# Taking the offset of the third normalisation on GpSimd instead of VectorE, one operation per tile of rows

## The chip, the cores and the metric

The kernel runs on one core of one Trainium2 chip. The metric is the time of one launch on the device, in microseconds (us). The kernel before has a median of 659.78 us in three runs (659.73 to 660.92). Engines are named as the profile names them: PE is TensorE (PEld its weight loads), DVE is VectorE, ACT is ScalarE, POOL is GpSimd, SP is the engine whose queue issues nearly all transfers.

## The reference, cut to what matters

A block of a transformer over 32 batches of 256 rows with 256 columns. An attention part of the mLSTM kind (8 heads, gates with cumulative sums, decay matrices) is added to x, and then a feed-forward part, which is where the third normalisation stands:

```python
x = x + tanh(g_xattn[0]) * L0_xattn_ref(layernorm(x), ctx_1024, ctx_1024, ...)   # ends in a second normalisation
x = x + tanh(g_ffn[0]) * L0_ffn_ref(layernorm(x), W_fc, W_proj)                  # layernorm(x): the third one
# layernorm(x) = (x - mean) / sqrt(var + 1e-5)
# L0_ffn_ref:  h = square(relu(x @ W_fc.T));  y = h @ W_proj.T;  five steps of a spiking neuron on y, mean of the spikes
```

## The kernel before, in words

A batch is 256 rows, kept as two tiles of 128 rows (`ST` is 2). Every engine has an order of work written out by hand: a start, and then a loop over `n in SLOTS` (n = 1 to 9), each turn of which handles four batches; I call one turn a slot. Work for a batch that doesn't exist is skipped, so that the last slots are partly empty. Engines wait for one another only on semaphores, and each engine works strictly in its own order: an instruction that waits holds up all that is behind it on its engine.

The third normalisation of batch b takes these steps. `x1_step` (DVE) makes x after the attention part. `ln3_stats` (DVE, L904) takes mean and variance into `mv3`. `ln3_rstd` (ACT, L915) makes 1/std of both tiles in two small activations (L370 and L371). `ln3_offset` (L926) makes minus mean times 1/std: on DVE, one instruction on 128x2 elements through `offset_of` (L374), which the first normalisation uses as well, on 128x4. `ln3_apply` (ACT, L934) makes the normalised rows `x1ln` with two activations (L942), which read the offset as their bias. `x2_T` (PE, L463) transposes them, `x2_hi_step` (ACT, L962) and `x2_lo_step` (DVE, L968) split them in two parts, and the feed-forward products follow: `z_step` (PE, L997), `relu_step` (ACT, L1007), `square` (ACT, L1019 and L1020), `square_lo` (POOL, L1040), `y_step` (PE, L1057), `spikes_step` (DVE, L1071 and L1075).

Other steps that the prediction speaks of:

- `am_split(n + 3, 0 to 3)` splits the gate rows of the next four batches in three bf16 parts: steps 0 and 2 on ACT (L635), steps 1 and 3 on POOL (L637). Only when step 3 (`am_part`) is done does SP go on with `load_a_rows` and `load_m_rows` (L650, six small transfers a batch).
- SP's order behind them in a slot is: rows for batches 4n+4 and 4n+5, `load_values(4n + 5)`, `stack_heads(4n + 5)` (L513, eight transfers that stack the heads of q and k), `load_k` and `load_values`, rows for 4n+6, `load_k`, `stack_heads(4n + 6)`, and then a store. (The last lines of one slot and the first of the next.)
- On POOL `k_hi(4n + 10)` (L428) waits until `stack_heads(4n + 6)` has landed, since it writes over what that reads. Behind it on POOL stand `v_lo_step(4n + 5)` (L456), `square_lo(2n + 1, 7)` (L1040) and `c_lo_step(4n + 5, 1)` (L746).
- `state(4n + 5)` (PE, L808) waits for `v_lo_step(4n + 5)`. `arg(4n + 6, 1)` (PE, L702) waits for the activation `decay_exp(4n + 6, 0)` (ACT, L728), which stands on ACT behind `ln3_apply(4n + 4)` and `x2_hi_step(4n + 3)`.
- `c_lo_step` (POOL, L746), `k_lo`, `k_weigh` and `state_lo` (POOL) are further elementwise work of the attention part.

Of the kernel before, what the change touches and what calls it, by code (L numbers as in the profile page):

```python
# [34 lines left out]
def build_block(nc, x, ctx_rows, ctx_cols, g_both, gate_w, gate_b, ln_scale, w_fc_t, w_proj_t, out):  # L35
# [37 lines left out]
    with ExitStack() as ctx:  # L73
# [852 lines left out]
        def ln3_offset(e, b):  # L926
            if not 0 <= b < B:
                return
            e.wait_ge(sem("ln3_rstd"), b + 1)
            if b - 2 >= 0:  # L930
                e.wait_ge(sem("x1ln"), b - 1)
            offset_of(e, off3[b % 2], mv3[b % 2], rstd3[b % 2]).then_inc(sem("ln3_offset"), 1)

        def ln3_apply(e, b):  # L934
            if not 0 <= b < B:
# [475 lines left out]
        def vector_program(e):  # L1411
            setup_rows(e, 1)
            setup_cols(e)
            ln1_stats(e, 0)
            ln1_stats(e, 1)
            ln1_offset(e, 0)
            setup_gates(e)
            ln1_stats(e, 2)
            q_lo(e, 0)
            q_lo(e, 1)  # L1420
            ln1_stats(e, 3)
            setup_rows(e, 0)
            gate_pre(e, 0)
            gate_cumsum(e, 0)
            ln1_offset(e, 1)
            gate_cummax(e, 0)
            ln1_stats(e, 4)
            am_split(e, 0, 1)
            ln1_stats(e, 5)
            am_split(e, 0, 3)  # L1430
            split_wfc_lo(e, 0)
            gate_pre(e, 1)
            setup_own(e)
            gate_cumsum(e, 1)
            gate_cummax(e, 1)
            q_lo(e, 2)
            am_split(e, 1, 1)
            ln1_offset(e, 2)
            q_lo(e, 3)
            cmul(e, 0, 0)  # L1440
            cmul(e, 0, 1)
            am_split(e, 1, 3)
            cmul(e, 0, 2)
            state_own(e, 0)
            ln1_stats(e, 6)
            q_lo(e, 4)
            split_wpr_lo(e, 0)
            split_wfc_lo(e, 1)
            cmul(e, 0, 3)
            gate_pre(e, 2)  # L1450
            gate_cumsum(e, 2)
            cmul(e, 1, 0)
            gate_cummax(e, 2)
            h_norm(e, 0)
            ln2_stats(e, 0)
            cmul(e, 1, 1)
            x1_step(e, 0)
            cmul(e, 1, 2)
            state_own(e, 1)
            ln3_stats(e, 0)  # L1460
            q_lo(e, 5)
            ln3_offset(e, 0)
            cmul(e, 1, 3)
            ln1_stats(e, 7)
            split_wpr_lo(e, 1)
            x2_lo_step(e, 0)
            ln1_offset(e, 3)
            cmul(e, 2, 0)
            h_norm(e, 1)
            cmul(e, 2, 1)  # L1470
            ln2_stats(e, 1)
            q_lo(e, 6)
            cmul(e, 2, 2)
            x1_step(e, 1)
            ln3_stats(e, 1)
            state_own(e, 2)
            cmul(e, 2, 3)
            ln3_offset(e, 1)
            ln1_stats(e, 8)
            q_lo(e, 7)  # L1480
            h_norm(e, 2)
            x2_lo_step(e, 1)
            ln2_stats(e, 2)
            cmul(e, 3, 0)
            x1_step(e, 2)
            cmul(e, 3, 1)
            gate_pre(e, 3)
            gate_cumsum(e, 3)
            gate_cummax(e, 3)
            ln1_stats(e, 9)  # L1490
            ln3_stats(e, 2)
            ln3_offset(e, 2)
            state_own(e, 3)
            cmul(e, 3, 2)
            ln1_offset(e, 4)
            spikes_step(e, 0, 0)
            spikes_step(e, 0, 1)
            cmul(e, 3, 3)
            spikes_step(e, 0, 2)
            spikes_step(e, 0, 3)  # L1500
            x2_lo_step(e, 2)
            spikes_step(e, 0, 4)
            cmul(e, 4, 0)
            h_norm(e, 3)
            cmul(e, 4, 1)
            ln2_stats(e, 3)
            cmul(e, 4, 2)
            x1_step(e, 3)
            cmul(e, 4, 3)
            q_lo(e, 8)  # L1510
            out_step(e, 0)
            for n in SLOTS:
                state_own(e, 4 * n)
                ln3_stats(e, 4 * n - 1)
                cmul(e, 4 * n + 1, 0)
                ln3_offset(e, 4 * n - 1)
                h_norm(e, 4 * n)
                ln2_stats(e, 4 * n)
                cmul(e, 4 * n + 1, 1)
                q_lo(e, 4 * n + 5)  # L1520
                x1_step(e, 4 * n)
                cmul(e, 4 * n + 1, 2)
                ln3_stats(e, 4 * n)
                cmul(e, 4 * n + 1, 3)
                ln3_offset(e, 4 * n)
                ln1_stats(e, 4 * n + 6)
                state_own(e, 4 * n + 1)
                x2_lo_step(e, 4 * n - 1)
                ln1_stats(e, 4 * n + 7)
                spikes_step(e, 2 * n - 1, 0)  # L1530
                cmul(e, 4 * n + 2, 0)
                spikes_step(e, 2 * n - 1, 1)
                ln1_offset(e, 2 * n + 3)
                x2_lo_step(e, 4 * n)
                spikes_step(e, 2 * n - 1, 2)
                spikes_step(e, 2 * n - 1, 3)
                spikes_step(e, 2 * n - 1, 4)
                cmul(e, 4 * n + 2, 1)
                out_step(e, 2 * n - 1)
                h_norm(e, 4 * n + 1)  # L1540
                q_lo(e, 4 * n + 6)
                ln2_stats(e, 4 * n + 1)
                cmul(e, 4 * n + 2, 2)
                x1_step(e, 4 * n + 1)
                ln3_stats(e, 4 * n + 1)
                state_own(e, 4 * n + 2)
                cmul(e, 4 * n + 2, 3)
                ln1_stats(e, 4 * n + 8)
                ln3_offset(e, 4 * n + 1)
                q_lo(e, 4 * n + 7)  # L1550
                h_norm(e, 4 * n + 2)
                cmul(e, 4 * n + 3, 0)
                ln2_stats(e, 4 * n + 2)
                gate_pre(e, n + 3)
                gate_cumsum(e, n + 3)
                gate_cummax(e, n + 3)
                x2_lo_step(e, 4 * n + 1)
                x1_step(e, 4 * n + 2)
                ln3_stats(e, 4 * n + 2)
                state_own(e, 4 * n + 3)  # L1560
                cmul(e, 4 * n + 3, 1)
                ln3_offset(e, 4 * n + 2)
                ln1_stats(e, 4 * n + 9)
                spikes_step(e, 2 * n, 0)
                spikes_step(e, 2 * n, 1)
                cmul(e, 4 * n + 3, 2)
                spikes_step(e, 2 * n, 2)
                spikes_step(e, 2 * n, 3)
                spikes_step(e, 2 * n, 4)
                cmul(e, 4 * n + 3, 3)  # L1570
                ln1_offset(e, 2 * n + 4)
                x2_lo_step(e, 4 * n + 2)
                out_step(e, 2 * n)
                cmul(e, 4 * n + 4, 0)
                h_norm(e, 4 * n + 3)
                cmul(e, 4 * n + 4, 1)
                ln2_stats(e, 4 * n + 3)
                cmul(e, 4 * n + 4, 2)
                x1_step(e, 4 * n + 3)
                cmul(e, 4 * n + 4, 3)  # L1580
                q_lo(e, 4 * n + 8)
# [228 lines left out]
        def gpsimd_program(e):  # L1810
# [31 lines left out]
            c_lo_step(e, 1, 2)  # L1842
            state_lo(e, 1)
            k_hi(e, 6)
            k_lo(e, 6)
            k_weigh(e, 2)
            c_lo_step(e, 1, 3)
# [7 lines left out]
            square_lo(e, 0, 1)  # L1855
            c_lo_step(e, 2, 2)
            state_lo(e, 2)
            c_lo_step(e, 2, 3)
            k_lo(e, 7)
            square_lo(e, 0, 2)  # L1860
# [9 lines left out]
            square_lo(e, 0, 6)  # L1870
            am_split(e, 3, 1)
            c_lo_step(e, 3, 1)
            am_split(e, 3, 3)
            square_lo(e, 0, 7)
            k_weigh(e, 4)
# [14 lines left out]
            k_hi(e, 9)  # L1890
            state_lo(e, 4)
            k_lo(e, 8)
            square_lo(e, 1, 3)
            v_lo_step(e, 5)
            v_hi_step(e, 6)
# [6 lines left out]
            c_lo_step(e, 5, 1)  # L1902
            square_lo(e, 1, 6)
            square_lo(e, 1, 7)
            c_lo_step(e, 5, 2)
            c_lo_step(e, 5, 3)
            k_weigh(e, 6)
# [15 lines left out]
            c_lo_step(e, 6, 3)  # L1923
            k_weigh(e, 7)
            for n in SLOTS:
                square_lo(e, 2 * n, 3)
                v_lo_step(e, 4 * n + 3)
                square_lo(e, 2 * n, 4)
# [3 lines left out]
                square_lo(e, 2 * n, 7)  # L1932
                am_split(e, n + 3, 1)
                c_lo_step(e, 4 * n + 3, 0)
                am_split(e, n + 3, 3)
                c_lo_step(e, 4 * n + 3, 1)
                square_lo(e, 2 * n + 1, 0)
# [16 lines left out]
                c_lo_step(e, 4 * n + 4, 3)  # L1954
                state_lo(e, 4 * n + 4)
                k_weigh(e, 4 * n + 5)
                k_hi(e, 4 * n + 9)
                c_lo_step(e, 4 * n + 5, 0)
                v_hi_step(e, 4 * n + 5)
# [5 lines left out]
                k_hi(e, 4 * n + 10)  # L1965
                v_lo_step(e, 4 * n + 5)
                square_lo(e, 2 * n + 1, 7)
                c_lo_step(e, 4 * n + 5, 1)
                c_lo_step(e, 4 * n + 5, 2)
                state_lo(e, 4 * n + 5)  # L1970
# [74 lines left out]
```

## Time and profile before

| what | us |
|---|---|
| median of three runs | 659.78 |
| the profiled execution itself | 662.98 |
| its span, first to last instruction | 661.2 |
| PE busy | 589.5 (89%) |
| DVE busy | 542.4 (82%) |
| POOL busy | 485.6 (73%) |
| ACT busy | 484.4 (73%) |
| chain that ended last, share of PE, DVE, ACT, POOL | 51%, 10%, 7%, 7% |
| the same, SP's queue, transfers, issue | 4%, 2%, 10% |

The granted clock of PE was 0.972 on average over the span. All rows of the trace come from the profiled execution, 3.2 us longer than the median. In a timeline a row is: start in us, duration in us, engine, line, operation, output and inputs, shapes, how many; in square brackets the idle time of the engine before it, and what ended that. In this profile a POOL instruction's duration overlaps the next one's start by some 0.04 us when they follow without a gap.

### The profile page before, as it was taken

How to read it: one execution, taken by the hardware profiler on the slowest of the kernel's cores; microseconds unless marked ns; L12 is line 12 of the kernel's file. 1: busy time of each engine (PE TensorE's matmuls, PEld its weight loads, DVE VectorE, ACT ScalarE, POOL GpSimd, SP SyncE). 2: the span in 40 equal slices, each digit the busy share in tenths (PEclk: the TensorE clock that was granted, in tenths of full speed). 3: DMA queues.
4: the chain of work that ended last, by engine and by line, in shares of the span. 5: the costliest groups of instructions: out<-in, count | busy, mean ns of one | idle time of the engine just before them, and what ended most of it. 6: DMA issues, size and time to landing. Idle time of an engine off the chain costs nothing.

```text
span 661.2 us, 17665 instructions
## 1 busy us (share of the span) xinstructions
PE 589.5 (89%) x6032; PEld 483.9 (73%) x6032; DVE 542.4 (82%) x1222; ACT 484.4 (73%) x1011; POOL 485.6 (73%) x531
## 2 busy tenths in 40 slices
PE   1265887799999999999999999999999999999795
PEld 0155776778787878787788878787878777787684
DVE  4878787889989998899989998999888998958522
ACT  4555777678787888788878878788878867676463
POOL 6157678867996969787897799787969788675232
PEclk9996799999999999999999999999999999999898
DMA  8915553845276335916573538642680556300000
GB/s 262 225 52 115 97 115 70 176 83 96 83 156 169 74 91 147 208 26 139 115 186 60 96 110 155 159 86 80 150 207 18 97 101 148 63 2 33 1 33 32
DMA packets 73192, 71.33 MB, mean 108 GB/s; under 512 B 8720, under 2 KB 68752, under 8 KB 73104
## 3 DMA queue, kind: packets, MB, share of 16 engines
q1 hardware_dynamic: 71888, 70.00, 47.3%
q8 instruction: 49, 0.80, 0.6%
q14 instruction: 39, 0.32, 0.2%
q10 hardware_dynamic: 1216, 0.21, 0.2%
HBM read 27.44 MB, written 8.39 MB: 54 GB/s over the span
## 4 chain that ended last, share of the span: by engine, by line
PE 51%; DVE 10%; issue 10%; ACT 7%; POOL 7%; SPq 4%; DMA 2%; POOLq 0%; ACTq 0%; DVEq 0%
PE z_ps L997 16%; PE y_ps L1057 16%; PE arg_ps L702 3%; PE qk_ps L717 3%; POOL sq_lo L1040 3%; DVE spikes L1075 3%; PE misc_ps L463 2%; SPq L650 2%; PE misc_ps L529 2%; SPq L513 2%; ACT sq_hi L1019 1%; POOL c_lo L746 1%; PE pv_ps L766 1%; PE pv_ps L764 1%; PE pv_ps L841 1%
## 5 line engine op out<-in xcount | busy, mean ns | idle before, releaser
L1040 POOL TENSOR_TENSOR sq_lo<-w_raw,sq_hi 128x512 fp32r<-128x512 f32 (+1 forms) x96 | 113.0, 1178 | 66.2 <-ACT w_raw L1020 66.1
L746 POOL TENSOR_TENSOR c_lo<-decay 128x512 bf16<-128x512 f32 x128 | 132.5, 1042 | 22.4 <-DVE decay L736 22.2
L997 PE MATMUL z_ps<-x_hi,wfc_hi 128*128 128x512 f32 (+1 forms) x288 | 115.7, 402 | 5.9 <-ACT w_raw L1007 4.1
L1057 PE MATMUL y_ps<-sq_hi,wpr_hi 128*128 128x512 f32 (+1 forms) x288 | 115.1, 400 | 1.1 <-POOL sq_lo L1040 1.1
L997 PE MATMUL z_ps<-x_hi,wfc_lo 128*128 128x512 f32 (+1 forms) x288 | 107.2, 372 | 0.0
L997 PE MATMUL z_ps<-x_lo,wfc_hi 128*128 128x512 f32 (+1 forms) x288 | 107.2, 372 | 0.0
L1057 PE MATMUL y_ps<-sq_lo,wpr_hi 128*128 128x512 f32 (+1 forms) x288 | 106.8, 371 | 0.0
L1057 PE MATMUL y_ps<-sq_hi,wpr_lo 128*128 128x512 f32 (+1 forms) x288 | 106.6, 370 | 0.0
L736 DVE TENSOR_TENSOR decay<-qk_ps,decay 128x512 f32<-128x512 f32 x128 | 87.1, 680 | 18.5 <-PE qk_ps L717 14.4
L728 ACT ACTIVATE decay<-arg_ps,lqk_col 128x512 f32<-128x512 f32 x128 | 86.5, 676 | 19.7 <-PE arg_ps L705 19.1
L1040 POOL TENSOR_TENSOR sq_lo<-relu,sq_hi 128x512 fp32r<-128x512 f32 (+1 forms) x48 | 56.3, 1173 | 37.9 <-ACT relu L1020 35.2
L1075 DVE SCALAR_TENSOR_TENSOR spikes<-y_ps,spikes 128x1024 bf16<-128x1024 f32 (+1 forms) x72 | 79.4, 1103 | 1.7
L1007 ACT ACTIVATE w_raw<-z_ps 128x512 f32<-128x512 f32 (+1 forms) x96 | 52.4, 545 | 29.6 <-PE z_ps L997 28.7
L997 PEld LDWEIGHTS z_ps<-x_hi,wfc_hi 128*128 128x128 f32 x288 | 55.0, 191 | 17.5 <-ACT w_raw L1007 4.8
L997 PEld LDWEIGHTS z_ps<-x_hi,wfc_lo 128*128 128x128 f32 x288 | 55.0, 191 | 10.0
L1057 PEld LDWEIGHTS y_ps<-sq_hi,wpr_lo 128*128 128x128 f32 x288 | 54.5, 189 | 10.0
L1057 PEld LDWEIGHTS y_ps<-sq_hi,wpr_hi 128*128 128x128 f32 x288 | 54.6, 190 | 9.4 <-POOL sq_lo L1040 2.1
L1019 ACT ACTIVATE sq_hi<-w_raw 128x512 fp32r<-128x512 f32 (+1 forms) x96 | 55.9, 582 | 6.2 <-PE y_ps L1057 5.3
L997 PEld LDWEIGHTS z_ps<-x_lo,wfc_hi 128*128 128x128 f32 x288 | 55.2, 192 | 6.7
L1057 PEld LDWEIGHTS y_ps<-sq_lo,wpr_hi 128*128 128x128 f32 x288 | 54.8, 190 | 6.4
L1020 ACT ACTIVATE w_raw<-w_raw 128x512 f32<-128x512 f32 (+1 forms) x96 | 56.3, 587 | 3.0
L702 PE MATMUL arg_ps<-m_rows,a_rows 128*128 128x128 bf16 x512 | 51.8, 226 | 5.7 <-ACT decay L728 5.2
(139 smaller groups left out, 1686.2 us busy)
## 6 DMA issues: line engine op xcount, KB each, us to landing
x_in<-x SPq DMA_DIRECT2D x32, 256.0 KB, 3.5
kT_in<-ctx_cols SPq DMA_DIRECT2D x32, 256.0 KB, 3.8
v_in<-ctx_rows SPq DMA_DIRECT2D x32, 256.0 KB, 3.2
k_stack<-kT_hi SPq DMA_DIRECT2D x64, 128.0 KB, 3.4
k_stack<-kT_lo SPq DMA_DIRECT2D x64, 128.0 KB, 3.7
q_stack<-qT_hi SPq DMA_DIRECT2D x64, 128.0 KB, 4.0
q_stack<-qT_lo SPq DMA_DIRECT2D x64, 128.0 KB, 4.2
out<-w_raw SPq DMA_DIRECT2D x32, 256.0 KB, 3.6
```

Of the source, the lines that this page charges most:

```text
L702: e.matmul(arg_ps[:, cols], a_rows[b % NAM][:, h, tok], m_rows[b % NAM][:, h, tok], start=(cols.start == 0), stop=False, skip_group_check= ...
L717: ins = e.matmul(qk_ps[:, cols], k_stack[slot][:, g, c, tok], q_stack[slot][:, g, c, tok], start=True, stop=True)
L728: e.activation(decay[i % NUN][:, :], arg_ps[:, :], ACT.Exp, bias=lqk_col[:, :]).then_inc(sem("decay"), 1)
L736: e.tensor_tensor(decay[i % NUN][:, :], qk_ps[:, :], decay[i % NUN][:, :], ALU.mult).then_inc(sem("cmul"), 1)
L746: e.tensor_tensor(c_lo[i % NCH][:, :], c, top(c), ALU.subtract).then_inc(sem("c_lo"), 1)
L997: ins = e.matmul(z_ps[:, tokens(q)], lhsT, rhs, start=(n == 0), stop=(n == len(terms) - 1))
L1007: e.activation(relu[n % NRE][:, tokens(q)], z_ps[:, tokens(q)], ACT.Relu).then_inc(sem("relu"), 1)
L1019: link(e, "scalar", e.activation(sq_hi[n % NSQ][:, tokens(q)], r, ACT.Square))
L1020: e.activation(r, r, ACT.Square).then_inc(sem("square"), 1)
L1040: e.tensor_tensor(sq_lo[n % NSQ][:, tokens(q)], relu[n % NRE][:, tokens(q)], sq_hi[n % NSQ][:, tokens(q)].bitcast(fp32), ALU.subtract).the ...
L1057: ins = e.matmul(y[:, c, :], w[:, j, c * P:(c + 1) * P], h, start=(j == 0 and i == 0 and (c == 0 or whole)), stop=(j == FT - 1 and i == 2) ...
L1075: ins = e.scalar_tensor_tensor(count, y, THETA[n], count, ALU.is_gt, ALU.add)
```

## The change

`ln3_offset` leaves DVE's order and goes into POOL's. Its one instruction on 128x2 becomes one `tensor_scalar` per tile of rows, each on 128x1, with 1/std as a per-partition scalar. What it waits for stays the same: 1/std of its batch, and the `x1ln` of two batches ago. The diff, shortened where slots repeat the pattern:

```diff
@@ ln3_offset
             e.wait_ge(sem("ln3_rstd"), b + 1)
             if b - 2 >= 0:
                 e.wait_ge(sem("x1ln"), b - 1)
-            offset_of(e, off3[b % 2], mv3[b % 2], rstd3[b % 2]).then_inc(sem("ln3_offset"), 1)
+            for t in range(ST):
+                ins = e.tensor_scalar(off3[b % 2][:, t:t + 1], mv3[b % 2][:, t, 0:1], rstd3[b % 2][:, t:t + 1], -1.0,
+                                      ALU.mult, ALU.mult)
+            ins.then_inc(sem("ln3_offset"), 1)
@@ vector_program: all seven calls go, three in the start and four in the loop
                 ln3_stats(e, 4 * n - 1)
                 cmul(e, 4 * n + 1, 0)
-                ln3_offset(e, 4 * n - 1)
                 h_norm(e, 4 * n)
...
                 state_own(e, 4 * n + 3)
                 cmul(e, 4 * n + 3, 1)
-                ln3_offset(e, 4 * n + 2)
@@ gpsimd_program, start
             k_hi(e, 6)
+            ln3_offset(e, 0)
             k_lo(e, 6)
...
             am_split(e, 3, 1)
             c_lo_step(e, 3, 1)
+            ln3_offset(e, 2)
             am_split(e, 3, 3)
...
@@ gpsimd_program, loop
             for n in SLOTS:
+                ln3_offset(e, 4 * n + 1)
                 square_lo(e, 2 * n, 3)
...
                 am_split(e, n + 3, 1)
                 c_lo_step(e, 4 * n + 3, 0)
+                ln3_offset(e, 4 * n + 2)
                 am_split(e, n + 3, 3)
                 c_lo_step(e, 4 * n + 3, 1)
...
                 state_lo(e, 4 * n + 4)
                 k_weigh(e, 4 * n + 5)
+                ln3_offset(e, 4 * n + 3)
                 k_hi(e, 4 * n + 9)
...
                 k_hi(e, 4 * n + 10)
                 v_lo_step(e, 4 * n + 5)
                 square_lo(e, 2 * n + 1, 7)
+                ln3_offset(e, 4 * n + 4)
                 c_lo_step(e, 4 * n + 5, 1)
```

In DVE's order the calls were for batches 0, 1 and 2 in the start and for 4n-1, 4n, 4n+1 and 4n+2 in the loop; in POOL's they are for batches 0 to 4 in the start and for 4n+1 to 4n+4 in the loop.

## Rows read from the trace of the kernel before

**Rows 1.** Groups by line and form: busy us, mean ns | idle us before, releaser.
```profile
L428 POOL TENSOR_SCALAR kT_hi<-kT_in 128x512 bf16<-128x512 f32 x32 | 21.0, 656 | 27.1 <-DMA kT_in<-ctx_cols 14.9 <-DMA q_stack<-qT_lo 12.2
...
L374 DVE SCALAR_TENSOR_TENSOR off<-mv,rstd 128x2 f32<-128x2 f32 x32 | 19.0, 593 | 6.5 <-ACT rstd L371 6.4
```
**Rows 2.** Groups of POOL by form, for the fixed part of an instruction.
```profile
L746 POOL TENSOR_TENSOR c_lo<-decay 128x512 bf16<-128x512 f32 x128 | 132.5, 1042 | 22.4 <-DVE decay L736 22.2
...
L794 POOL TENSOR_TENSOR kw_lo<-kw 128x256 bf16<-128x256 f32 x32 | 20.1, 629 | 0.2
...
L2039 POOL MEMSET const-bfloat16-1.0<- 128x1 bf16 x1 | 0.1, 102 | 0.0
```
**Rows 3.** Timeline of POOL around am_part in slots 3 and 4.
```profile
310.42 1.03 POOL L746 TENSOR_TENSOR c_lo<-decay 128x512 bf16<-128x512 f32 x1
311.42 1.16 POOL L637 TENSOR_TENSOR am_part<-am_rest,am_part 32x512 bf16<-32x512 f32 x1
...
315.00 1.28 POOL L1040 TENSOR_TENSOR sq_lo<-w_raw,sq_hi 128x512 fp32r<-128x512 f32 x1 [1.42 <-ACT w_raw L1020]
...
382.54 1.16 POOL L637 TENSOR_TENSOR am_part<-am_rest,am_part 32x512 bf16<-32x512 f32 x1
```
**Rows 4.** Timeline of ACT, 1/std and x1ln of batch 4n+2 in slot 3.
```profile
311.34 0.21 ACT L371 ACTIVATE rstd<-lnv 128x2 f32<-128x2 f32 x1
...
312.63 1.10 ACT L942 ACTIVATE x1ln<-x,off,rstd 128x256 f32<-128x256 f32 x2 [0.44 <-DVE off L374]
```
**Rows 5.** Timeline of DVE, the offsets of batch 0 and of 4n+2 in slot 3.
```profile
65.28 0.38 DVE L374 SCALAR_TENSOR_TENSOR off<-mv,rstd 128x2 f32<-128x2 f32 x1 [1.09 <-ACT rstd L371]
...
311.57 1.02 DVE L374 SCALAR_TENSOR_TENSOR off<-mv,rstd 128x2 f32<-128x2 f32 x1 [0.19 <-ACT rstd L371]
```
**Rows 6.** Timeline of SP's queue, slot 3: first and last of the rows of 38 issues.
```profile
312.64 2.12 SPq L650 DMA_DIRECT2D a_rows<-am_part  x3
...
337.57 1.25 SPq L513 DMA_DIRECT2D q_stack<-qT_lo  x2
```
**Rows 7.** Timeline of POOL, slot 3, from k_hi(4n+10) on.
```profile
342.76 0.62 POOL L428 TENSOR_SCALAR kT_hi<-kT_in 128x512 bf16<-128x512 f32 x1 [1.34 <-DMA q_stack<-qT_lo]
343.34 1.12 POOL L456 TENSOR_TENSOR v_lo<-v_in,v_hi 128x512 bf16<-128x512 f32 x1
344.43 1.27 POOL L1040 TENSOR_TENSOR sq_lo<-relu,sq_hi 128x512 fp32r<-128x512 f32 x1
345.66 2.04 POOL L746 TENSOR_TENSOR c_lo<-decay 128x512 bf16<-128x512 f32 x2
```
**Rows 8.** Timeline of PEld: inter, state and arg in slot 3.
```profile
319.73 0.10 PEld L841 LDWEIGHTS pv_ps<-state_f,qT_hi 128*128 128x128 bf16 x1 [0.59 <-POOL s_lo L829]
...
344.54 0.10 PEld L808 LDWEIGHTS pv_ps<-v_hi,kw 128*128 128x128 bf16 x1
...
348.15 0.23 PEld L702 LDWEIGHTS arg_ps<-m_rows,a_rows 128*128 128x128 bf16 x4 [0.28 <-issue]
```
**Rows 9.** Timeline of ACT, x1ln of batch 4n+4 in slots 3 and 5.
```profile
345.75 1.10 ACT L942 ACTIVATE x1ln<-x,off,rstd 128x256 f32<-128x256 f32 x2 [0.82 <-DVE off L374]
...
488.68 1.10 ACT L942 ACTIVATE x1ln<-x,off,rstd 128x256 f32<-128x256 f32 x2 [1.32 <-DVE off L374]
```
**Rows 10.** Timeline of PEld: state and arg in slot 5.
```profile
487.47 0.10 PEld L808 LDWEIGHTS pv_ps<-v_hi,kw 128*128 128x128 bf16 x1 [0.61 <-issue]
...
490.95 0.24 PEld L702 LDWEIGHTS arg_ps<-m_rows,a_rows 128*128 128x128 bf16 x4 [0.31 <-issue]
```
**Rows 11.** Timeline of POOL, slot 5: v_lo and what follows it.
```profile
486.28 1.12 POOL L456 TENSOR_TENSOR v_lo<-v_in,v_hi 128x512 bf16<-128x512 f32 x1
487.36 1.27 POOL L1040 TENSOR_TENSOR sq_lo<-w_raw,sq_hi 128x512 fp32r<-128x512 f32 x1
```
**Rows 12.** Timeline of POOL in the start and in slot 7.
```profile
71.73 1.04 POOL L746 TENSOR_TENSOR c_lo<-decay 128x512 bf16<-128x512 f32 x1 [2.79 <-DVE decay L736]
...
613.55 1.29 POOL L1040 TENSOR_TENSOR sq_lo<-relu,sq_hi 128x512 fp32r<-128x512 f32 x1 [1.50 <-ACT relu L1020]
```

More of the change, by code:

```diff
@@ L1461, in vector_program @@
             q_lo(e, 5)
-            ln3_offset(e, 0)
             cmul(e, 1, 3)
@@ L1477, in vector_program @@
             cmul(e, 2, 3)
-            ln3_offset(e, 1)
             ln1_stats(e, 8)
@@ L1491, in vector_program @@
             ln3_stats(e, 2)
-            ln3_offset(e, 2)
             state_own(e, 3)
@@ L1524, in vector_program @@
                 cmul(e, 4 * n + 1, 3)
-                ln3_offset(e, 4 * n)
                 ln1_stats(e, 4 * n + 6)
@@ L1548, in vector_program @@
                 ln1_stats(e, 4 * n + 8)
-                ln3_offset(e, 4 * n + 1)
                 q_lo(e, 4 * n + 7)
@@ L1857, in gpsimd_program @@
             state_lo(e, 2)
+            ln3_offset(e, 1)
             c_lo_step(e, 2, 3)
@@ L1892, in gpsimd_program @@
             k_lo(e, 8)
+            ln3_offset(e, 3)
             square_lo(e, 1, 3)
@@ L1904, in gpsimd_program @@
             square_lo(e, 1, 7)
+            ln3_offset(e, 4)
             c_lo_step(e, 5, 2)
```

## The prediction, made before the changed kernel was run

> **What bounds the kernel now.** I read the page first: the chain that ended last is half PE, with 10% DVE, 7% ACT and 7% POOL, so PE sets the time but is handed short waits by the others. Then the groups by form. The offset on DVE is 128x2 elements, yet costs 593 ns on average, 19.0 us in all [rows 1]; the reader is to see that it starts at 311.57 and ends at 312.59, with POOL's am_part at 312.58 [rows 3, 5]. That looks like a price that the change takes away. So the third view was the timeline of each engine over one slot (n = 3, from about 297 to 368 us), and there the question was which wait is passed from slot to slot.
>
> A slot is 71.12 us long (am_part at 311.42 and at 382.54 [rows 3]). The loop that closes on itself is this. When am_part ends at 312.58, SP starts at 312.64 and issues 38 transfers one behind the other, with gaps of at most 0.12 us, until the last of stack_heads(4n+6) at 338.82 [rows 3, 6]. That lands at about 342.7, and k_hi(4n+10) on POOL had waited 1.34 us for it [rows 7]. Behind it stands v_lo(4n+5), which ends at 344.46, and at 344.54 PE starts state(4n+5) [rows 7, 8]. In slot 5 v_lo ends at 487.40 and state starts at 487.47, after 0.61 us in which PE's loads had stood [rows 10, 11]. From there PE works without a gap into the gate transposes, and ACT and POOL take it to the next am_part. So am_part is on the loop, and a delay of it is passed on one to one, because SP has nothing to give back. This holds for n = 1 to 5: in slot 6 batch 34 doesn't exist, so nothing waits for the transfers, and from slot 7 on there is no am_part.
>
> **The price of one new instruction.** Call it c, from start to start. The trace has no 128x1 tensor_scalar on POOL. Two elementwise forms differ in width alone: 1042 ns at 512 elements and 629 ns at 256 [rows 2], which is 1.61 ns an element and 216 ns at none; less the 0.04 us by which neighbours overlap that is 0.18 us. Bounds from both sides: 0.10 us, a memset of 128x1 [rows 2], and 0.62 us, the tensor_scalar on 512 elements, 656 ns less 0.04 [rows 1]. I take 0.18, since the operation reads and writes as those two do; 0.30 I hold possible for the per-partition scalar.
>
> The Trainium skill, "GPSIMD Engine Reference", section "Performance pitfalls for Q7 kernels", says that many small read commands cost about 102 cycles each and do not overlap. At the 1.2 GHz of the same page that is an estimate of 0.085 us for each of the two reads here; if they came on top of half the fixed price, c would be near 0.27 and the sum below 6.0 us in place of 4.2. No row shows a POOL instruction this small that reads, so I leave it in the upper half of the range.
>
> **Part 1, offset(4n+2) before am_part.** POOL reaches it when c_lo ends, at 311.42 in slot 3. But 1/std ends at 311.55 [rows 4], and DVE, which was waiting for it, started at 311.57 [rows 5]; POOL can start at about 311.6. Then two instructions, then am_part: it starts 0.18 + 2c later, 0.54 us. Queued behind it on POOL are c_lo(4n+3,1) and square_lo(2n+1,0); the latter had an idle of 1.42 us before it [rows 3], so these lose nothing. What isn't covered is am_part itself, and through it SP. Five slots: 0.90 + 10c = 2.7 us.
>
> **Part 2, offset(4n+4) behind square_lo(2n+1,7).** On DVE it ran beside POOL's work; on POOL it comes when square_lo is done, at 345.66 [rows 7]. It ends at 345.66 + 2c + 0.04, and with 0.05 us to reach ACT, x1ln(4n+4) starts at 345.75 + 2c, where it was 345.75 [rows 9]. In slot 5 the start is 487.36 + 1.23 + 0.09 + 2c = 488.68 + 2c, where it was 488.68 [rows 9, 11]. Late next on ACT are x_hi and the decay, and for that decay PE's arg(4n+6,1) waits: 2.27 us after x1ln in slot 5, with 0.31 us of standing [rows 9, 10]. In slot 3 arg started at 348.15, 2.40 us after x1ln, so 0.13 us are spare [rows 8, 9]. Price: 2c in slot 5, 2c - 0.13 in slot 3; I take the mean, 2c - 0.07, for each of five slots: 10c - 0.3 = 1.5 us. This lies behind state on PE, and so adds to part 1.
>
> **Part 3, the other two of each slot.** Offset(4n+1) and offset(4n+3) find 1/std ready or within 0.1 us, and push POOL by 2c = 0.36 us. The second is covered by the 1.34 us for which k_hi(4n+10) waits anyway [rows 7], the first by a wait of square_lo for ACT, of the kind of the 1.42 us [rows 3]. Nothing; without that cover each would cost 0.36 us a slot, 1.8 us over five.
>
> **Part 4, start and end.** In the start offset(0) holds POOL from about 64.4 until 1/std is there at about 65.3 [rows 5], and k_lo(6), k_weigh(2) and c_lo(1,3) behind it move by 0.9 + 2c, some 1.2 us; an idle of 2.79 us before 71.73 takes that in [rows 12]. In slot 7 offset(31) makes square_lo(15,5) wait for 1/std of the last batch, some 0.9 us; before the next square_lo stands an idle of 1.50 us [rows 12]. I count nothing for both, and 1.2 and 0.9 us if the cover fails.
>
> **Part 5, what DVE gets back.** 19.0 us of busy time and 6.5 us of waits [rows 1]. None of it is on the loop above, where DVE doesn't stand between am_part and state. x1ln(4n+2) gets earlier, by the 0.44 us that ACT had waited [rows 4], but what comes of it is used on PE before state, where PE now has time to spare. Nothing.
>
> **The sum.** 0.90 + 10c + 10c - 0.3 = 0.6 + 20c, with c = 0.18 4.2 us. The profiled execution took 662.98 us, so 667.2; times 659.78 / 662.98 = 0.9952 for the median, 664.0 us. With c = 0.10 the sum is 2.6 and the time 662.4; with 0.30, 6.6 and 666.4; with 0.62, 13.0 and 672.7.
>
> **Rival A, faster.** The place is s_lo before inter(4n+3): PE stood 0.59 us for it [rows 8], and it hangs on square_lo(2n+1,0), which hangs on ACT behind x1ln(4n+2). The offset was blocked on DVE for the rest of am_part (1.02 us for 128x2 [rows 5]); on POOL it ends at 311.6 + 0.40 = 312.0, and x1ln starts 0.44 us earlier [rows 4]. If that decided in six slots, it would be 2.6 us: 657.2. For it speaks that the printed chain goes this way; against it that in slots 3 and 5 state starts within 0.08 us of v_lo's end, which has nothing to do with x1ln. It decides if the transfers land by their own queue and not by when SP issued them. The block is what the Trainium skill, "SBUF — State Buffer", section "Who interferes with whom", states: a DVE instruction with two SBUF inputs contends with a GpSimd instruction that reads SBUF, and the second to start waits for all of the first. The trace agrees [rows 3, 5]; by this rule alone the change gains.
>
> **Rival B, no change.** The delay of am_part is absorbed between SP and POOL: the last transfer took 3.9 us from its issue to k_hi [rows 6, 7], and if transfers queue there, an issue 0.5 us later may land at the same time. Then only part 2 is left, and against it part of rival A's gain: between -1 and +1.2 us, about 659.8.
>
> **Rival C, much slower.** A POOL instruction with a per-partition scalar costs as much as a wide one, or the cover of part 3 fails: 668 to 673. Against it, that no group of POOL shows a fixed price over 0.2 us.
>
> **Rival D**, the change doesn't do what it says: DVE's offset gone, yet x1ln starting no later or earlier anywhere. The two tiles' offsets are the same numbers, and I see no way to it; 1%, as no change.
>
> **Chances.** Forecast (c from 0.10 to 0.35) 64%, rival A 11%, rival B 14%, rival C 10%, D 1%. Changes within 0.2%, 1.3 us, are about what a measurement of this kernel can't tell from none. Of the forecast nearly all lies above that, and a part of B lies on either side. Slower by over 0.2%: 0.74; within 0.2%: 0.14; faster: 0.12. The forecast's own range is 662.4 to 667.3; the range for 8 times in 10 reaches down through half of B and up into C: 659.4 to 668.6.
>
> **What would show it right or wrong.** Right: POOL has 64 instructions on 128x1 of 0.2 us; am_part starts 0.4 to 0.7 us later after the end of the c_lo before it; the slots are 71.9 to 72.1 us long; k_hi(4n+10) still waits for the transfers; PEld stands 0.3 us or more before state in slots 1 to 5. DVE's busy time falls by some 19 us without use. Wrong: slots of 71.1 us or less, state starting well behind v_lo's end, or the last stack transfer landing where it did relative to the slot.

## The result and the profile after

The changed kernel takes 665.41 us (median of 8 runs, 664.17 to 667.13), the kernel before on the same chips 660.70 (8 runs, 659.73 to 663.89). The ratio is 1.0065, with an interval of 1.0044 to 1.0086, so 4.3 us slower (2.9 to 5.7). The forecast was 664.0, with 4.2 us of difference.

The span of its profiled execution is 665.3 us. From the page of the changed kernel: busy times, the new group on POOL, and the chain that ended last.

```profile
PE 591.3 (89%) x6032; PEld 484.4 (73%) x6032; DVE 526.8 (79%) x1190; ACT 483.5 (73%) x1011; POOL 501.7 (75%) x595
...
PE 32%; SPq 20%; DVE 11%; issue 10%; POOL 7%; ACT 6%; DMA 5%; POOLq 0%; ACTq 0%; DVEq 0%
```

```profile
L933 POOL TENSOR_SCALAR off<-mv,rstd 128x1 f32<-128x1 f32 x64 | 16.0, 265 | 3.9 <-ACT rstd L371 3.4
```

DVE is 15.6 us less busy, and the kernel is slower. POOL has 64 new instructions in 16.0 us, and SP's queue has 20% of the printed chain, where it had 4%.

POOL and ACT in slot 3, the answer to [rows 3, 4, 5]:

```profile
312.80 1.03 POOL L746 TENSOR_TENSOR c_lo<-decay 128x512 bf16<-128x512 f32 x1
314.01 0.50 POOL L933 TENSOR_SCALAR off<-mv,rstd 128x1 f32<-128x1 f32 x2 [0.18 <-ACT rstd L371]
314.47 1.16 POOL L637 TENSOR_TENSOR am_part<-am_rest,am_part 32x512 bf16<-32x512 f32 x1
```
```profile
314.55 1.10 ACT L945 ACTIVATE x1ln<-x,off,rstd 128x256 f32<-128x256 f32 x2
```

The wait is 0.18 us as worked out, and the two instructions take 0.46 us from start to start, so c is 0.23. Am_part starts 1.67 us after c_lo where it was 1.00. ACT no longer waits for the offset.

POOL and ACT behind v_lo(4n+5) in slots 3 and 4, the answer to [rows 7, 9]:

```profile
345.88 0.62 POOL L428 TENSOR_SCALAR kT_hi<-kT_in 128x512 bf16<-128x512 f32 x1 [1.53 <-DMA q_stack<-qT_lo]
346.47 1.11 POOL L456 TENSOR_TENSOR v_lo<-v_in,v_hi 128x512 bf16<-128x512 f32 x1
347.54 1.27 POOL L1043 TENSOR_TENSOR sq_lo<-relu,sq_hi 128x512 fp32r<-128x512 f32 x1
348.79 0.51 POOL L933 TENSOR_SCALAR off<-mv,rstd 128x1 f32<-128x1 f32 x2
...
418.61 1.11 POOL L456 TENSOR_TENSOR v_lo<-v_in,v_hi 128x512 bf16<-128x512 f32 x1
```
```profile
349.33 1.10 ACT L945 ACTIVATE x1ln<-x,off,rstd 128x256 f32<-128x256 f32 x2 [2.09 <-POOL off L933]
...
421.48 1.10 ACT L945 ACTIVATE x1ln<-x,off,rstd 128x256 f32<-128x256 f32 x2 [1.96 <-POOL off L933]
```

And the same place of slot 4 in the kernel before, which the prediction had not read (DVE, POOL and ACT):

```profile
416.12 0.16 DVE L374 SCALAR_TENSOR_TENSOR off<-mv,rstd 128x2 f32<-128x2 f32 x1
```
```profile
415.08 1.12 POOL L456 TENSOR_TENSOR v_lo<-v_in,v_hi 128x512 bf16<-128x512 f32 x1
416.16 1.27 POOL L1040 TENSOR_TENSOR sq_lo<-w_raw,sq_hi 128x512 fp32r<-128x512 f32 x1
```
```profile
416.31 1.10 ACT L942 ACTIVATE x1ln<-x,off,rstd 128x256 f32<-128x256 f32 x2 [0.23 <-DVE off L374]
```

In the changed kernel x1ln(4n+4) starts 1.75 us after v_lo's end in slot 3 and 1.76 in slot 4. Before it was 1.29 in slot 3 (345.75 less 344.46, [rows 7, 9]), where DVE's offset stood until square_lo ended, but only 0.11 in slot 4: there the offset started 0.04 us before square_lo and got through. In slots 2 and 5 it was 1.28, much as in slot 3. In slot 1 it was 0.05: DVE's offset had stood there too, but only until v_lo ended.

**A cleaner measure than the time.** Executions of one kernel scatter by 3 to 8 us from the lowest to the highest, so I cut each slot in two at the end of v_lo(4n+5). Stretch A goes from there to the end of the next am_part, stretch B from the end of am_part to v_lo. In the changed kernel A is 40.38, 40.36, 40.38, 40.38 and 40.39 us, in the kernel before 38.83, 39.28, 39.24, 38.78 and 39.26. There it has two levels, 38.8 and 39.26, 0.45 us apart: the lower one in slots 1 and 4, where x1ln(4n+4) starts at most 0.11 us after v_lo's end, and the upper one where DVE's offset(4n+4) stands until square_lo ends. B scatters, since transfers stand in it. Between the two profiled executions A takes 5 x 1.30 = 6.5 us more, B 5 x 0.70 = 3.5 less, am_part of slot 1 ends 2.5 later, and the rest behind slot 6's is 1.4 shorter: together 4.1, the difference of the spans.

### The profile page after: what moved, and what is told of

Read it like the earlier page. It is cut to its first block, busy times and chain, and to the rows that moved or that the text cites. A ratio compares the mean times of both kernels' runs of the same rounds, so it can differ in the third digit from the quotient of the medians.

```text
span 665.3 us, 17697 instructions
## 1 busy us (share of the span) xinstructions
PE 591.3 (89%) x6032; PEld 484.4 (73%) x6032; DVE 526.8 (79%) x1190; ACT 483.5 (73%) x1011; POOL 501.7 (75%) x595
## 4 chain that ended last, share of the span: by engine, by line
PE 32%; SPq 20%; DVE 11%; issue 10%; POOL 7%; ACT 6%; DMA 5%; POOLq 0%; ACTq 0%; DVEq 0%
PE z_ps L1000 11%; SPq L650 10%; PE y_ps L1060 10%; SPq L513 8%; DVE spikes L1078 6%; DMA q_stack<-qT_lo 4%; POOL sq_lo L1043 2%; PE arg_ps L702 2%; PE qk_ps L717 2%; DVE spikes L1074 1%; PE misc_ps L529 1%; ACT sq_hi L1022 1%; POOL am_part L637 1%; DVE stat L358 1%; ACT x1ln L945 1%
```

## The experiments

The times are differences to the kernel before on the same chip. Each is the ratio on record of the two kernels' runs, less one, times the median before, with its 95% interval; it can differ by up to 1.4 us from the plain difference of the two medians. Most of the intervals reach 1.2 to 1.9 us to either side, so that differences between two rows of the table are less certain than the rows. A and B are means over slots 1 to 5 of one profiled execution each.

| kernel | against before, us | A | B |
|---|---|---|---|
| before | 0 | 39.08 | 32.38 |
| the change | +4.3 (2.9 to 5.7) | 40.38 | 31.68 |
| part 1 alone | +1.9 (0.4 to 3.3) | 39.47 | 32.06 |
| delay of part 1, no offset moved | +1.0 (-0.7 to 2.6) | 39.84 | 31.56 |
| part 2 alone | +3.4 (2.2 to 4.7) | 39.75 | 32.24 |
| change without part 2 | +1.6 (0.3 to 2.9) | 39.73 | 31.77 |
| part 3 alone | -0.5 (-1.5 to 0.5) | 39.32 | 31.94 |
| change, start on DVE | +5.6 (3.7 to 7.5) | 40.36 | 31.83 |
| change, 4n+2 behind am_part | +3.8 (2.4 to 5.3) | 39.77 | 31.96 |
| change, one instruction | +1.1 (-0.3 to 2.6) | 39.72 | 31.65 |
| before, k_hi behind v_lo | +0.3 (-1.3 to 2.0) | 42.14 | 29.93 |
| change, k_hi behind v_lo | +3.0 (1.3 to 4.7) | 42.44 | 29.83 |
| before, two instructions on DVE | -2.0 (-3.1 to -0.8) | 39.08 | 32.33 |
| before, offset on ACT | +7.0 (5.4 to 8.7) | 40.45 | 31.71 |

**Offset(4n+2) behind am_part.**

```diff
                 c_lo_step(e, 4 * n + 3, 0)
-                ln3_offset(e, 4 * n + 2)
                 am_split(e, n + 3, 3)
+                ln3_offset(e, 4 * n + 2)
```

> As the change, but offset(4n+2) stands behind am_part on POOL. The trace of the change gives c = 0.23 us for one new instruction, and its am_part starts 0.64 us (0.18 of wait and 2c) behind the c_lo before it, in five slots that count. Theory (the loop over am_part, SP, the stack transfers and v_lo): 5 x 0.64 = 3.2 us of the change's 4.3 to 4.7 go away, so about 1.2 us above the kernel before. x1ln(4n+2) then starts some 0.7 us later than before, and that must cost nothing. Rival 1 (every new instruction on POOL costs its own length wherever it stands): no gain, 4.5 us above the kernel before. Rival 2 (x1ln(4n+2) leads to s_lo and the inter product on PE): the gain is eaten, 3 us or more above before.

It came out 3.8 us slower than before, no gain that can be measured. A falls by 0.61 as expected, but B grows by 0.28, and POOL in slot 3 shows why:

```profile
344.16 0.62 POOL L428 TENSOR_SCALAR kT_hi<-kT_in 128x512 bf16<-128x512 f32 x1 [0.28 <-PE misc_ps L529]
```

K_hi no longer waits for the transfers here: in slots 3 to 5 they have landed when POOL comes. X1ln(4n+2) starts 1.67 us after am_part's start, where it was 1.21, and what hangs on it brings POOL late by itself. The theory's 1.2 us is refuted. The time fits rival 2, and the trace shows its way: a second chain is nearly as long as the one over SP. Rival 1's 4.5 us lies inside the interval too; it falls with the kernels that follow.

**Part 1 alone, part 2 alone, the change without part 2, part 3 alone.** These call one function with the POOL form (`_g`) or one with the old DVE form (`_v`), each at the place of its engine. Where engines alternate, each waits for the offset of the batch before:

```diff
+            if b - 1 >= 0:
+                e.wait_ge(sem("ln3_offset"), b)
@@ part 1 alone, gpsimd_program; all others stay ln3_offset_v on DVE
+                ln3_offset_g(e, 4 * n + 2)
@@ part 2 alone, gpsimd_program, and ln3_offset_g(e, 4) in the start
+                ln3_offset_g(e, 4 * n + 4)
@@ the change without part 2, vector_program
+                ln3_offset_v(e, 4 * n)
@@ part 3 alone, gpsimd_program, and ln3_offset_g(e, 3) in the start
+                ln3_offset_g(e, 4 * n + 1)
...
+                ln3_offset_g(e, 4 * n + 3)
```

> As the kernel before, but offset(4n+2) alone is taken on POOL, in front of am_part; all others stay on DVE. Theory: 5 x (0.18 + 2 x 0.23) = 3.2 us slower than before. Rival 1 (each new instruction costs its length anywhere, 4.5 us over 64 of them): 16 of 64, 1.1 us. Rival 2 (the earlier x1ln pays the delay back): 1 us or less, or a gain.

> Only the offsets of batches 4, 8, 12, ... are on POOL, behind square_lo(2n+1,7); all others stay on DVE. This is the missing corner beside part 1 alone, both, and part 3 alone. I measure with the stretch from the end of v_lo(4n+5) to the end of the next am_part, which repeats to some 0.02 us in five slots: 39.08 us before on average, 40.38 after, 39.47 with part 1 alone. Theory (the two parts lie one behind the other on one path): 40.38 less the 0.64 of part 1, so 39.74 in every slot, 0.66 above before, and the time 2 to 3.3 us above before. Rival (the parts overlap, and each alone costs nearly what both do): 40.0 or more and over 3.5 us. Second rival (part 2 matters only when part 1 has made the rest late): 39.3 or less and under 1 us.

> As the change, but the offsets of batches 4, 8, 12, ... (4n+4) are back on DVE at their old place. Theory: part 2 goes away, 5 x 2 x 0.23 - 0.3 = 2.0 us, so about 2.5 us above the kernel before. Rival 1 (by share of instructions): 8 of 32 batches, 1.1 us less, 3.4 above before. Rival 3 (the path behind v_lo has slack of its own for x1ln(4n+4)): no gain, 4.5 above before.

> Only the offsets of batches 3, 5, 7, 9, ... are on POOL, at the places of the change; batches 0, 1, 2 and all 4n+2 and 4n+4 stay on DVE. The prediction counted these at nothing. Theory: within 1 us of the kernel before (with 16 offsets of 0.46 us on POOL, 7.4 us of its time in all, hidden). Rival 1 (an instruction costs its length wherever it stands, 4.5 us for all 32 offsets): half of that, 2.2 us slower.

Part 1 alone cost 1.9 us, where 3.2 was expected; 3.2 lies just inside the interval. Part 2 alone cost 3.4, a little over its range, and its A was 39.75, where 39.74 stood in the expectation. Without part 2 the change costs 1.6 us. Part 3 costs nothing that shows: 15 offsets of 0.46 us lie under waits of POOL. Rival 1, by which an instruction on POOL costs its length anywhere, falls with this: it gave part 2 1.1 us and part 3 2.2, and both lie outside the intervals.

Part 1 alone also moved DVE's offset(4n+4) to another place beside POOL's work. In its trace x1ln(4n+4) starts at most 0.14 us after v_lo's end in all five slots, where in the kernel before that was so in two. So A is at 39.5 throughout, 0.67 above the lower level, but only 0.39 above the mean before. This is slot 2, where the offset had taken 0.79 us before:

```profile
274.54 0.16 DVE L374 SCALAR_TENSOR_TENSOR off<-mv,rstd 128x2 f32<-128x2 f32 x1
```

**The delay without the offset.**

```diff
+        def hold(e, b):
+            e.wait_ge(sem("ln3_rstd"), b + 1)
+            for t in range(ST):
+                e.tensor_scalar(idle2[:, t:t + 1], eps_col[:, :], eps_col[:, :], -1.0, ALU.mult, ALU.mult)
@@ gpsimd_program
+                hold(e, 4 * n + 2)
                 am_split(e, n + 3, 3)
```

> As the kernel before, with all offsets on DVE, but in front of am_part POOL waits for 1/std of batch 4n+2 and runs two tensor_scalar on 128x1 that write a tile which nothing reads. So it has the delay of part 1 and nothing of what DVE gets back. Theory: 3.2 us slower than before, the same as with the real offset there. Rival 2 (what DVE gets back is worth something): this kernel is slower than the one with the real offset, by up to 5 x 0.44 = 2.2 us.

1.0 us, with zero inside the interval and 3.2 outside it, so the delay isn't passed on one to one. But the kernel isn't the delay alone. While POOL waits for 1/std, DVE's offset(4n+2) gets through in front of am_part. It took 1.02 us before, and here in slot 3:

```profile
312.39 0.16 DVE L375 SCALAR_TENSOR_TENSOR off<-mv,rstd 128x2 f32<-128x2 f32 x1
```

X1ln(4n+2) starts 0.02 us before am_part, about as early as with the real offset on POOL (0.08 us behind am_part's start). So this kernel has what DVE gets back as well, and it can't tell rival 2 from the theory. What speaks against a worth of it at this place is the changed kernel's trace: square_lo(2n+1,0) starts 4.10 us after the c_lo before am_part in slot 3, where it was 4.58, and k_hi(4n+10) then waits for the transfers all the same.

**The start back on DVE.**

```diff
@@ the change, vector_program: batches 0, 1 and 2; they go from gpsimd_program
+            ln3_offset_v(e, 0)
...
+            ln3_offset_v(e, 1)
...
+            ln3_offset_v(e, 2)
```

> As the change, but the offsets of batches 0, 1 and 2, in the start, are back on DVE. In the trace of the change am_part of slot 1 is 2.5 us late, where the prediction had counted nothing for the start. Theory: that is real and is kept to the end, so this kernel is some 2 us below the change and 2.5 above before. Rival: it is absorbed later by the waits for the transfers (from am_part to v_lo the change's trace is 0.7 us shorter in a slot): less than 0.7 us below the change.

5.6 us above before (6 runs), so not clearly below the change, and the theory's 2.5 is refuted. That the 2.5 us at slot 1 in the trace of the change are a cost of the start's offsets isn't shown. Over the traces of all the kernels am_part of slot 1 ends between 167.9 and 172.2, and the latest is the kernel with part 2 alone, which has the offsets of batches 0 to 3 on DVE.

**One instruction in place of two.**

```diff
-            for t in range(ST):
-                ins = e.tensor_scalar(off3[b % 2][:, t:t + 1], ...
+            e.tensor_tensor(off3[b % 2][:, :], mv3[b % 2][:, :, 0], rstd3[b % 2][:, :], ALU.mult)
```

> As the change, but POOL makes the offset by one tensor_tensor on 128x2 in place of two tensor_scalar on 128x1; the minus sign is left out. Theory: one instruction of this size costs about 0.25 us, so 0.21 us are saved at each of the two places of a slot, 2.1 us in five slots and 0.4 in the start: about 2 us below the change. Rival (the wait for 1/std and the order, not the length, is the loss): within 0.7 us of the change.

The instruction took 0.15 us from start to start:

```profile
309.92 0.20 POOL L932 TENSOR_TENSOR off<-mv,rstd 128x2 f32<-128x2 f32 x1 [0.17 <-ACT rstd L371]
310.07 1.16 POOL L637 TENSOR_TENSOR am_part<-am_rest,am_part 32x512 bf16<-32x512 f32 x1
```

That is 0.31 less at each of the two places of a slot, and A fell by 0.66. Five slots make 3.3 us, and the time is 3.2 below the change's. So the loss in A scales with the length of these instructions. B stays at 31.65, although am_part is now delayed by 0.33 us and no longer by 0.64.

**K_hi(4n+10) behind v_lo(4n+5)**, in the kernel before and in the changed one.

```diff
-                k_hi(e, 4 * n + 10)
                 v_lo_step(e, 4 * n + 5)
+                k_hi(e, 4 * n + 10)
```

> As the kernel before, but k_hi(4n+10), which waits for the stack transfers of 4n+6, stands behind v_lo(4n+5) on POOL and not in front of it. Theory (the loop over the transfers sets the slot): v_lo(4n+5) no longer waits 1.3 to 2.5 us, state(4n+5) on PE starts up to the 0.6 to 1.2 us earlier for which PE's loads had stood, and five slots give 2 to 3.5 us, so 2 to 3.5 us faster than before. Rival (another chain of nearly the same length, over x1ln(4n+2) and square_lo, holds the slot, as the kernel with the offset behind am_part seems to show): within 1 us of before.

> As the change, with the same move: k_hi(4n+10) behind v_lo(4n+5). Theory: the 0.64 us of delay of am_part per slot is no longer passed on through v_lo to PE's state, and offset(4n+4) comes about 1 us earlier in the slot, since square_lo(2n+1,7) in front of it is reached earlier; 3 to 4 us less than the change, so 0.5 to 1.5 us above the kernel before. Rival (the delay goes on by ACT's x1ln and POOL's own order, not by the transfers): no more than 1 us less than the change, 3.5 us above before.

No gain in the first, and none that is clear in the second. Slots 1 and 2 did get shorter in the first (71.05 and 70.87 us, before 72.01 and 71.22), but slots 4 and 5 took 73.3. The move takes v_lo and PE's state out from behind the transfers, but not square_lo(2n+1,7) and what follows on POOL: in slots 1, 4 and 5 k_hi still waits 1.01, 0.88 and 0.99 us for the transfers, in slots 2 and 3 under 0.1. Who waited for what on PE in slot 4 (us in all, times, longest):

```profile
PEld qk_ps L717 <- issue: 3.9, 12, 1.0
...
PEld y_ps L1086 <- DVE spikes L1075: 1.2, 1, 1.2
```

State(4n+5) no longer stands, but a product of q_stack and k_stack now has an idle of 0.98 us before it, and a `y` product waits 1.2 us for the spikes. In the kernel before PE is busy 70.4 to 70.8 us of each such slot of 71.1 to 72.0, so the gate that the prediction saw was one of several, mostly with less than 1 us between them.

**The form of the change on DVE.**

```diff
@@ the kernel before, ln3_offset, still called on DVE
-            offset_of(e, off3[b % 2], mv3[b % 2], rstd3[b % 2]).then_inc(sem("ln3_offset"), 1)
+            for t in range(ST):
+                ins = e.tensor_scalar(off3[b % 2][:, t:t + 1], mv3[b % 2][:, t, 0:1], rstd3[b % 2][:, t:t + 1], -1.0,
+                                      ALU.mult, ALU.mult)
+            ins.then_inc(sem("ln3_offset"), 1)
```

> As the kernel before, all offsets on DVE at their places, but in the form of the change: two tensor_scalar on 128x1 in place of one scalar_tensor_tensor on 128x2. It tells form from engine. Theory: the loss is POOL's in-order queue and not the form, so this is not slower than before; if one tensor input in place of two keeps DVE from waiting for POOL's running instruction, an offset costs some 0.3 us in all in place of 0.59 on average, x1ln(4n+2) and x1ln(4n+4) start 0.3 to 0.5 us earlier, and it is 1 to 3 us faster than before. Rival (the two instructions are blocked as the one was): same as before within 0.7 us or slower, with a mean of about 0.6 us for the pair.

2.0 us faster than before by the ratio of the runs (0.8 to 3.1); the medians are 659.44 us (11 runs) and 662.29 before. This version beats both kernels. The group, and the activations x1ln(4n+2) of slot 3:

```profile
L933 DVE TENSOR_SCALAR off<-mv,rstd 128x1 f32<-128x1 f32 x64 | 10.5, 205 | 7.6 <-ACT rstd L371 7.3
```
```profile
313.61 1.08 ACT L945 ACTIVATE x1ln<-x,off,rstd 128x256 f32<-128x256 f32 x2
```

No single instruction took more than 0.22 us, where the one before went up to 1.26. X1ln(4n+2) starts 0.66 us after am_part's start, where it was 1.21. In slots 1, 4 and 5 A is 38.80 to 38.84, the lower of the two levels, but its mean is no lower than before, since slot 2 took 39.93: there 1/std itself came late. B is no shorter either (32.33, before 32.38). The profiled execution took 662.26 us, 2.8 more than this kernel's median, so that a trace of a typical execution, and with it the place where the 2.0 us are won, is missing. That it is the stopped offset(4n+4) is what A in the three slots suggests; it isn't shown.

**The offset on ACT.**

```diff
@@ ln3_stats, DVE
+            e.tensor_scalar(nm3[b % 2][:, :], mv3[b % 2][:, :, 0], -1.0, None, ALU.mult).then_inc(sem("ln3_neg"), 1)
@@ ln3_rstd, ACT
+            for t in range(ST):
+                ins = e.activation(off3[b % 2][:, t:t + 1], nm3[b % 2][:, t:t + 1], ACT.Identity,
+                                   scale=rstd3[b % 2][:, t:t + 1])
+            ins.then_inc(sem("ln3_offset"), 1)
```

> As the kernel before, but ACT makes the offset itself, by two activations on 128x1 (minus the mean, times 1/std as scale) right behind 1/std; DVE takes minus the mean behind its statistics. No engine is crossed between 1/std and x1ln. Theory: ACT had waited 0.44 us for DVE's offset in front of x1ln(4n+2) and 0.2 to 1.3 us in front of x1ln(4n+4); two activations take some 0.45 us, so about 0.4 us a slot are won and some 1 us of ACT's time a batch is added elsewhere under cover: 0 to 2 us faster than before. Rival (ACT's queue is on PE's way to work, as the short waits of PE for w_raw show): 1 to 3 us slower.

7.0 us slower. The two places in question are DVE's new instruction and ACT behind it, slot 3:

```profile
346.91 1.04 DVE L916 TENSOR_SCALAR nm<-mv 128x2 f32<-128x2 f32 x1
```
```profile
348.04 0.48 ACT L931 ACTIVATE off<-nm,rstd 128x1 f32<-128x1 f32 x2 [0.60 <-DVE nm L916]
```

The block came back: on 128x2 `tensor_scalar` took 1.04 us beside POOL's square_lo, and 0.48 us of ACT stand behind it. The edit also lets DVE wait for its own statistics before this instruction. How much of the 7 us is ACT's longer queue, how much this block and how much DVE's added work I haven't separated.

## Why the prediction was right, and where it wasn't

- **c.** Taken 0.18, measured 0.23, inside the bounds. The tensor_tensor with two small reads took 0.15 from start to start and 0.20 as recorded. The Trainium skill, "GPSIMD Engine Reference", section "Performance pitfalls for Q7 kernels", has about 102 cycles for each small read command, from which the prediction's estimate was 0.27 for c and 0.17 for two commands alone; these rows neither show such a price nor rule it out.
- **Part 1, the place.** Wait and delay came out as worked out: 0.18 + 2c = 0.64 us, in every slot. SP's first issue starts 0.06 us behind am_part in all slots of both kernels.
- **Part 1, the price.** "A delay of it is passed on one to one, because SP has nothing to give back" is the sentence that failed. With c = 0.23 it gave 3.2 us; alone it cost 1.9 (0.4 to 3.3), with the offset kept on DVE 1.0 (-0.7 to 2.6), and beside part 2 it adds 0.9 (4.3 less 3.4). Each is uncertain by itself; together they lie below 3.2. Two things come back. One is A: in the kernel with part 1 alone offset(4n+4) was not stopped by square_lo in any slot, so that A rose by 0.39 and not by 0.67. The other is B. I pooled B by whether am_part is delayed, over kernels that differ in other ways too (without: before, two instructions on DVE, part 2 alone, part 3 alone, 4n+2 behind am_part; with: the change, start on DVE, part 1 alone, without part 2, one instruction, delay only). It is 32.17 in 25 slots without and 31.76 in 30 slots with the delay, so 0.41 of the 0.64 us come back on average; single slots spread from 31.2 to 33.8 and from 30.7 to 32.9. All of it is in SP's 38 issues, 26.57 and 26.15 us on average, where the shortest take 25.3; from the last issue's end to k_hi it is 3.90 and 3.91. So SP does have something to give back: single issues take up to 1.4 us longer than their like, and in sum less where am_part is delayed. It doesn't follow the size of the delay: B is 31.65 with one instruction (0.33 us) and 31.68 with two (0.64). Why, the traces don't say, and I tried nothing on it. Rival B named this place, with the wrong reason (the landing).
- **Part 2.** Sized at 2c - 0.07 a slot, 2.0 us at c = 0.23, from slots 3 and 5. It cost 3.4 alone and 2.7 in the change (4.3 less 1.6). Slots 3 and 5 were both ones in which DVE's offset stood until square_lo ended; in slots 1 and 4 it didn't, and there x1ln(4n+4) got later not by 2c = 0.46 but by 1.70 and 1.64 us. In A part 2 alone costs 0.41 to 0.46 in slots 2 and 3, 0.67 in slot 5 and 0.88 and 0.95 in slots 1 and 4. So of the 1.64 us some 0.7 were covered, and of the 0.46 in slots 2 and 3 next to nothing.
- **The sum.** 0.6 + 20c with the true c is 5.2 us, and 4.3 were measured. That the forecast of 4.2 came so near is luck: part 1 was too dear, part 2 too cheap, and c too low. The mechanism, two delays on POOL that add up, is shown. The four kernels with neither, either and both parts (the one with neither being the kernel before) give 0, 1.9, 3.4 and 4.3 us, whose sum fits within the intervals, and A shows it without that noise: from the lower level, 38.81, it goes to 39.48 with part 1, 39.71 with part 2 (slots 1 to 4) and 40.38 with both, and 0.67 and 0.90 make 1.57.
- **Part 3** was nothing, as said. **Part 4** too, as far as the times can tell.
- **Part 5 and rival A.** What DVE gets back was said to be worth nothing, and no run shows a gain from it in this change. DVE is 15.6 us less busy, where about 19 were forecast. But the stopped offset did cost time in the kernel before: through x1ln(4n+4) A is 0.45 us longer in three slots of five, 1.4 us in all. With the form changed and the engine kept, the kernel is 2.0 us faster (0.8 to 3.1); whether this is the way of that gain, or rival A's over x1ln(4n+2) and s_lo has a part in it, stays open.
- **The closed loop** over the transfers is real in its pieces (k_hi waits 0.75 to 1.53 us for them in the changed kernel), but it isn't the only one of its length. The slots of the kernel before were not alike: 72.0, 71.2, 71.1, 71.3 and 71.7 us, and PE's loads stood before state 1.21, 0.14, 0.10, 0.69 and 0.61 us, where the prediction read only the last. In slots 2 and 3 PE's own work came nearly as late as v_lo. In the changed kernel slot 2 is again at 0.12, under the 0.3 that the prediction gave as a sign of being right. That the way over v_lo and state alone sets the slot is refuted by the two kernels with k_hi behind v_lo; that the transfers set it in part, through what stands on POOL behind k_hi, is not.

## What to carry to other kernels

An instruction that is stopped by another engine is a reason to look at its form before its engine: in this kernel two small instructions that weren't stopped beat one that was, and both beat the move to an engine that works in strict order and is itself waited for. When work is moved onto such an engine, count the places where the engine's next step is waited for, not the instructions: here 15 offsets cost nothing and 7 cost 3.4 us. Its length is the price at such a place only if the work had to wait for the same step before; where it had run beside it, as offset(4n+4) had in two slots, the price is more. And when a row repeats from slot to slot, read it in every slot before sizing a term by it: here two of five slots were at another level. An experiment that holds one engine back also lets the others through; read what it frees before calling it the delay alone.

## What the runs showed of the hardware that I had not expected

On DVE, an offset of 128x2 elements as a scalar_tensor_tensor took 0.13 to 1.26 us in the kernel before, the longest of them ending with a POOL instruction that ran beside it, and minus the mean, a tensor_scalar with one tensor input on 128x2, 0.17 to 1.26 us (588 ns on average over 32; 1.04 in the row above). The same arithmetic as the offset, as tensor_scalar on 128x1, took 179 to 217 ns in all 64 instances. So one tensor input isn't enough to stay clear.

The Trainium skill, "VectorE: DVE Perf Modes", section "Mode 2×_2P — use both read ports for one tensor", says that a single-source instruction in SBUF whose outermost dimension is even can use both read ports. The 128x2 tensor_scalar, with its 1.04 us beside square_lo, fits that, though no trace shows the mode itself. That an instruction with one element per partition stays out of it is my inference from the 64 instances; no run tests it otherwise.

A stopped instruction isn't always let in when the POOL instruction beside it ends. The offset of the first normalisation, a scalar_tensor_tensor on 128x4 that took 142 ns at its shortest, stood once in the start of the kernel with two instructions on DVE until five POOL instructions, one right behind the other, had passed:

```profile
101.35 3.34 DVE L374 SCALAR_TENSOR_TENSOR off<-mv,rstd 128x4 f32<-128x4 f32 x1
```

On POOL, a tensor_scalar on 128x1 with a per-partition scalar took 0.23 us from start to start (0.26 as recorded), a tensor_tensor on 128x2 0.15 (0.20 as recorded).
